# Flamingo block on one core: queries from a feature-major x, LayerNorm's factor applied after the product, and the bias added over two score banks at once

## The reference, cut to what matters

```python
x = x + tanh(g_xattn) * attention(layernorm(x), ctx, ctx, bias, Wq, bq, ..., Wk, ..., Wv, ...)
x = x + tanh(g_ffn) * experts(layernorm(x), Wg, bg, W1, b1, W2, b2)

layernorm(x) = (x - mean(x)) / sqrt(var(x) + 1e-5)          # over the 256 features
q = (layernorm(x) @ Wq' + bq) / 4;  k = ctx @ Wk' + bk;  v = ctx @ Wv' + bv     # LoRA merged into W'
scores = q @ k.T + bias          # bias: 16 heads x 128 x 128 for each sequence
p = softmax(scores);  out = p @ v
```

## Time and profile before

| | |
|---|---|
| time, median of 3 runs | 1283.33 us (1281.91 to 1287.55) |
| span of the profiled execution, first to last instruction | 1282.7 us |
| TensorE busy | 1264.4 us (99%) |
| VectorE busy | 1098.7 us (86%) |
| GpSimd busy | 1034.5 us (81%) |
| ScalarE busy | 860.4 us (67%) |
| mean granted TensorE clock | 0.998 |

### The profile page before, as it was taken

How to read it: one execution, slowest core, us unless ns; L and a number is a source line. 1 busy time by engine, 2 the same in 40 slices (tenths; PEclk the granted TensorE clock), 3 DMA queues, 4 the chain that set the end, 5 groups by cost and what they waited for, 6 DMA issues and landing times. The chain is left out here.

```text
span 1282.7 us, 42229 instructions
## 1 busy us (share of the span) xinstructions
PE 1264.4 (99%) x12820; PEld 1078.7 (84%) x12820; DVE 1098.7 (86%) x2504; ACT 860.4 (67%) x1916; POOL 1034.5 (81%) x1179
## 2 busy tenths in 40 slices
PE   8999999999999999999999999999999999999997
PEld 7888888888888888888888888888887788888886
DVE  6899999999999999999999999999999856665655
ACT  4777777777777777777777777777776533333332
POOL 4879989999999999999999999989988755544545
PEclk9999999999999999999999999999999999999999
DMA  6655655556655656555555555555655589888885
GB/s 237 213 179 196 193 187 181 188 186 196 191 185 181 186 187 197 191 192 183 181 185 187 195 193 185 181 184 187 192 195 182 187 271 282 281 278 281 276 281 184
DMA packets 110649, 263.48 MB, mean 205 GB/s; under 512 B 15332, under 2 KB 34278, under 8 KB 110464
## 3 DMA queue, kind: packets, MB, share of 16 engines
q1 hardware_dynamic: 96912, 226.76, 56.6%
q0 software_dynamic: 12624, 34.62, 6.9%
q10 hardware_dynamic: 1056, 1.39, 0.3%
HBM read 226.72 MB, written 36.91 MB: 206 GB/s over the span
## 5 line engine op out<-in xcount | busy, mean ns | idle before, releaser
L455 POOL TENSOR_TENSOR sc<-sc,negmax 128x1024 f32<-128x1024 f32 x256 | 482.4, 1901 | 25.6 <-DVE negmax L1029 20.7
L1023 DVE TENSOR_TENSOR sc<-bank,sc 128x512 f32<-128x512 f32 x512 | 328.2, 683 | 12.3 <-PE bank L560 7.5
L1029 DVE TENSOR_REDUCE negmax<-sc 128x8 f32<-128x1024 f32 x256 | 312.4, 1220 | 16.3
L862 ACT ACTIVATE PT<-bank 128x512 f32<-128x512 f32 x512 | 281.1, 607 | 1.7 <-PE bank L585 1.5
L585 PE MATMUL bank<-cst,sc 128*128 128x128 f32 x2048 | 272.6, 276 | 0.0
L585 PEld LDWEIGHTS bank<-cst,sc 128*128 128x128 f32 x2048 | 225.3, 140 | 25.8 <-issue 25.1
L525 POOL DMA_INDIRECT out<-og,ids x120 | 118.8, 990 | 114.7 <-issue 106.6
L856 ACT COPY OT<-bank 128x512 f32<-128x512 f32 x128 | 75.1, 587 | 152.1 <-PE bank L595 152.0
L510 POOL DMA_INDIRECT rows_dram<-x2n,slot_i x128 | 136.5, 1066 | 29.3 <-issue 25.2
L560 PE MATMUL bank<-KT,QT 32*128 32x256 f32 x2048 | 146.6, 400 | 0.6 <-ACT V L904 0.6
L595 PE MATMUL bank<-PT,V 128*32 128x128 f32 x4096 | 137.6, 275 | 0.3 <-issue 0.3
(11 more groups left out here) (148 smaller groups left out, 2052.0 us busy)
## 6 DMA issues: line engine op xcount, KB each, us to landing
sc<-in_bias SPq DMA_DIRECT2D x256, 512.0 KB, 4.9
w_sb<-in_w SPq DMA_DIRECT2D x69, 257.0 KB, 3.9
CT<-in_w SPq DMA_DIRECT2D x69, 256.0 KB, 4.1
xg<-rows_dram SPq DMA_DIRECT2D x63, 272.0 KB, 3.8
x_sb<-in_x SPq DMA_DIRECT2D x128, 128.0 KB, 2.0
CT<-in_ctx_in SPq DMA_DIRECT2D x64, 256.0 KB, 5.4
rows_dram<-x2n,slot_i POOLq DMA_INDIRECT x128, 3.8
out<-og,ids POOLq DMA_INDIRECT x120, 4.0
```

Source lines behind the costliest of these rows:

```text
L455: nc.gpsimd.tensor_tensor(s, s, m, ALU.add).then_inc(sub_ok, 1)
L862: nc.scalar.activation(PT[:, t.slot(2), 512 * q:512 * q + 512], turn_bank(t, q)[:], ACT.Exp).then_inc(pt_ready, 1)
L1023: nc.vector.tensor_tensor(s, b_s[q][:], s, ALU.add).then_inc(s_used, 1)
L1029: nc.vector.tensor_reduce(negmax[:, t.slot(2), 8 * h:8 * h + 8], sc[:, t.slot(4), 1024 * h:1024 * h + 1024].rearrange("p (h k) -> p h k", ...
```

## The change

- x is given a second time, feature-major (`x_turned`), and SP loads it straight into `XT`, one transfer of 256 KB for each pair of sequences. ScalarE's first `normalise`, TensorE's two transposes of `xn` and ScalarE's copy to `XT` go.
- The mean is taken out by the weights: once, at the start, the column means of the merged Wq are subtracted from it (two products with ones, one VectorE instruction).
- The factor rs of each token goes through DRAM: `send_scale` writes 128 numbers, `spread_scale` reads them back broadcast over the 128 partitions into `RS`. VectorE's new `scale_queries` multiplies the queries' product by it, from PSUM into `QT`, two instructions of 128x256 for each pair of sequences, behind the residual `x2` in even steps. ScalarE's `queries` then adds the bias in place, as the last thing in its step.
- `add_bias` works on two banks at once (`two[h]`, 128x1024): two instructions in a step in place of four.
- The values' product goes to bank 6. The scores of odd steps wait for `scaled_ok`, that is for `scale_queries` of the step before.

```diff
+            def send_scale(t):
+                sp.wait_ge(rs_ok, t.n(1, 1))
...
+                sp.dma_start(rs_dram[t.n()], ln[:, (t.k - 7) % 8, 0, 0:1]).then_inc(rs_out, 16)
+
+            def spread_scale(t):
+                pair = t.k // 2 % 2
...
+                sp.wait_ge(rs_out, t.n(16, 16))
...
+                sp.dma_start(RS[:, pair, tok:tok + P], rs_rows[t.n()].partition_broadcast(P)).then_inc(rs_in[pair], 16)
...
                 if cur:
                     pe.wait_ge(v_evac, val.n() if val else N)
+                    if ky and ky.slot(2) == 0:
+                        pe.wait_ge(scaled_ok, ky.per(2, 1, 1))
...
-                    pe.wait_ge(xt_evac, qry.n(1, 2))
+                    pe.wait_ge(xT_in[qry.k // 2 % 2], qry.per(4, 16, 16))
                     project("q", qry, XT[:, qry.k // 2 % 2], q_ready)
...
-                    if cur:
-                        pe.wait_ge(s_used, cur.n(4, 3))
-                    elif val.reached(1):
+                    if not cur and val.reached(1):
                         pe.wait_ge(v_evac, val.n())
                     for c in range(KC):
-                        ins = mm(b_v[:, 0:HID], CT[:, pair, c, tok:tok + P], W["v"][:, c, :],
+                        ins = mm(b_v, CT[:, pair, c, tok:tok + P], W["v"][:, c, :],
                                  start=(c == 0), stop=(c == KC - 1))
...
-                    for c in range(KC):
-                        ins = nc.tensor.transpose(b_x[:, c * P:c * P + P],
-                                                  xn[:, nxt.slot(2), c * P:c * P + P], ident)
-                    ins.then_inc(xt_ready, 1)
...
+                act.wait_ge(scaled_ok, t.per(2, 1, 1))
                 for o in range(KC):
-                    act.wait_ge(q_ready, t.per(2, KC, o + 1))
-                    ins = nc.scalar.activation(QT[:, pair, o, :], b_s[o][:, 0:2 * P],
+                    ins = nc.scalar.activation(QT[:, pair, o, :], QT[:, pair, o, :],
                                                ACT.Identity, bias=bq_col[:, o:o + 1])
...
-                dve.wait_ge(s_ready, t.n(4, q + 1))
-                s = sc[:, t.slot(4), 512 * q:512 * q + 512]
-                nc.vector.tensor_tensor(s, b_s[q][:], s, ALU.add).then_inc(s_used, 1)
+                dve.wait_ge(s_ready, t.n(4, 2 * h + 2))
+                s = sc[:, t.slot(4), 1024 * h:1024 * h + 1024]
+                nc.vector.tensor_tensor(s, two[h][:], s, ALU.add).then_inc(s_used, 2)
...
+            def scale_queries(t):
+                pair = t.k // 2 % 2
+                dve.wait_ge(rs_in[pair], t.per(4, 32, 32))
+                for o in range(KC):
+                    dve.wait_ge(q_ready, t.per(2, KC, o + 1))
+                    ins = nc.vector.tensor_tensor(QT[:, pair, o, :], b_s[o][:, 0:2 * P], RS[:, pair, :], ALU.mult)
+                ins.then_inc(scaled_ok, 1)
...
+                        if qry and qry.slot(2) == 0:
+                            scale_queries(qry)
```

More of the change, by code:

```diff
@@ L193, in flamingo_block @@
         inv = sb("inv", [P, 8, HALVES])
-        bank = [ctx.enter_context(nc.psum_tensor(f"bank{i}", [P, 512], F32)) for i in range(8)]
+        two = [ctx.enter_context(nc.psum_tensor(f"two{i}", [P, 1024], F32)) for i in range(2)]
+        bank = [two[i // 2][:, 512 * (i % 2):512 * (i % 2) + 512] for i in range(4)]
+        bank += [ctx.enter_context(nc.psum_tensor(f"bank{i}", [P, 512], F32)) for i in range(4, 8)]
         b_s, b_t = bank[0:4], bank[4:6]
         b_x, b_o = bank[6], bank[7]
-        b_v, b_x2 = b_s[2], b_s[3]
+        b_v, b_x2 = b_x[:, 0:HID], b_s[3]
         o_ps = b_o[:].rearrange("p (h c) -> p h c", c=CELL)
@@ L347, in _ @@
             load(cst[:, 0:C_FIRST], consts[:, 0:C_FIRST], s_id)
+            def send_scale(t):
+                sp.wait_ge(rs_ok, t.n(1, 1))
+                sp.nop(nofuse=True)
+                sp.dma_start(rs_dram[t.n()], ln[:, (t.k - 7) % 8, 0, 0:1]).then_inc(rs_out, 16)
+            def spread_scale(t):
+                pair = t.k // 2 % 2
+                if t.reached(4):
+                    sp.wait_ge(scaled_ok, t.per(2, 1, -1))
+                    sp.nop(nofuse=True)
+                sp.wait_ge(rs_out, t.n(16, 16))
+                sp.nop(nofuse=True)
+                tok = P * t.slot(2)
+                sp.dma_start(RS[:, pair, tok:tok + P], rs_rows[t.n()].partition_broadcast(P)).then_inc(rs_in[pair], 16)
             def step(i, k):
+                behind = seq(i, k, -4)
+                if behind and not (isinstance(i, int) and k < 0):
+                    send_scale(behind)
                 t = seq(i, k, -6) if k > FIRST else None
@@ L548, in _ @@
             pe.wait_ge(s_id, 16)
+            pe.wait_ge(s_cst, 16)
+            pe.wait_ge(s_setd, 3)
+            for c in range(KC):
+                ins = mm(bank[SETUP_BANKS[1]][:, 0:HID], cst[:, C_ONE:C_ONE + P], W["q"][:, c, :],
+                         start=(c == 0), stop=(c == KC - 1))
+            ins.then_inc(s_setc, 1)
             def scores(t):
@@ L586, in turn, with values @@
                 ins.then_inc(tr_ready, 1)
-            def values(t, nxt):
+            def values(t):
                 pe.wait_ge(pt_ready, t.n(4, 4))
-                pe.wait_ge(xt_evac, nxt.n() if nxt else N)
                 if not t.reached(1):
@@ L884, in step @@
                 if old:
[L885 to L887 removed]
+                    normalise(old)
                 if scored:
@@ L895, in step @@
                     copy_rows(early[k - N + 2])
-                if qry and qry.slot(2) == 0:
-                    queries(qry)
                 if ky and ky.slot(2) == 0:
@@ L1095, in step @@
                 if cur:
[L1096 to L1101 removed]
+                    for h in range(2):
+                        add_bias(cur, h)
+                        row_max(cur, h)
                 if here.reached(2) and (gate or done or grp):
@@ L1135, in step @@
                     aggregate(ahead, 0)
+                if qry and qry.slot(2) == 0 and not done:
+                    scale_queries(qry)
                 stats(done, 1)
@@ L1367 @@
     nc = bacc.Bacc("TRN2", target_bir_lowering=False, num_devices=1)
-    order = ["x", "ctx_in", "bias", "wqT", "wkT", "wvT", "bv", "lora_in", "w1", "w2", "b2",
+    order = ["x", "x_turned", "ctx_in", "bias", "wqT", "wkT", "wvT", "bv", "lora_in", "w1", "w2", "b2",
              "consts"]
```

102 lines of the change are left out of this document (49 added, 53 removed).

## The result

The changed kernel takes **2007.8 us** (median of four executions, 2005.3 to 2017.5); the kernel before took 1284.2 on the same chip (1281.9 to 1287.6). The ratio is 1.5645, 95% interval 1.5598 to 1.5692. The forecast was 1330, so the direction was right and 678 us of the 724 were missing from the sum. The profiled execution took 2008.2 us, its span 2006.4.

What follows compares the result with a forecast made beforehand. TensorE and VectorE were taken to share the bound within 1%. Own work +0.7 and waits 2.27 gave +2.97 us per eight steps, times 15.5, plus 2 for the start: 48 on 1282.7, so 1330 us; range given 1295 to 1350.

Steps and rivals of the forecast that it cites:

- Start and transfers: Kernel start and DRAM trip of the factors: +2 us at the start, bounds 0 and 6; in the loop, hidden.
- Rival 3: RS lands late: from 7 us on VectorE waits in every pair, 64 us per further microsecond, 1394 at 8 us; chance 0.06.
- transfers on SP's queue: Sign that the forecast is wrong: transfers on SP's queue appear as a wait of VectorE.
- The round trip: VectorE's scale to TensorE's odd scores to VectorE's next add: 1.35 us, bounds 1.23 and 1.39.
- The wait without routing: VectorE's stall for the scores of odd steps without routing: 0.76 us, in two odd steps of eight.
- With routing: VectorE's stall for odd scores where list_slots fills part of the trip: 0.20 us, in the other two odd steps.
- From odd to even: VectorE's wait between an odd add and the next even one, where TensorE's 7.31 us decides: 0.35 us, once in eight steps.
- The scale: VectorE's scale_queries between residual and statistics: 0.99 us where 0.53 stood, +1.84 in eight steps, bounds 1.6 and 2.2.
- The adds: VectorE's bias adds over two banks: 0.065 us saved a pair, 1.04 us in eight steps, bounds 0.5 and 1.2.
- term of 2 for the start: Centring of Wq and the DRAM trip ahead of the first keys' product: +2 us, bounds 0 and 6.
- Rival 1: TensorE alone is the bound and VectorE has room: 28 us go, 1255 us; chance 0.06.
- Rival 2: The VectorE-TensorE round trip is covered and only VectorE's own work counts: 1296 us; chance 0.08.

Runs made afterwards that it cites:

- e3: e1 with the write of 128 neighbouring 4-byte factors put back on SP's queue, nobody waiting for it or reading it: 1894.1 us.
- e5: e3 with the 128 unread 4-byte pieces put 512 bytes apart in DRAM: 1322.7 us.
- e11: e3 with the 128 unread 4-byte pieces put 64 bytes apart in DRAM: 1324.2 us.
- e6: e3 with 128 unread pieces of 512 bytes in place of 4 bytes, once a step: 1324.3 us.
- e1: The changed kernel without the factors' write to DRAM and SP's wait for it; RS is loaded from ones of the constants: 1321.7 us.
- e8: e1 with the scaling of the queries' product moved ahead of the reciprocal, directly behind the second reduction: 1321.3 us.
- e9: e1 without the scaling on VectorE, the odd scores' wait for it and the load of RS; ScalarE empties the queries' banks: 1274.7 us.
- e10: The kernel before with only the wide adds and the moved banks and wait for ScalarE's copy that they need: 1288.3 us.

## Why the prediction was wrong, point by point

**The step that failed: "Start and transfers".** It said: "In the loop the trip is issued more than a step ahead [...]; transfers land in 2.0 to 5.4 us. Hidden." Rival 3 had the trip late, by itself, at "64 us for each further microsecond" and 0.06. Both took the trip's time as a latency that either fits or doesn't, and priced the write by other transfers. The runs show something else in its place:

- The write has no fixed landing time to be hidden. With its 128 words as neighbours it takes 9.2 to 13.6 us in the chain; with the words 64 or 512 bytes apart it lands in 5.5 and 5.4. The prediction says itself that writes of 4 bytes a partition are not in the trace of before; it bounded the landing by the rows of that trace all the same.
- While it runs, the others run slow too: the x transfer 11.0 us instead of 2.0, GpSimd's scatter 9.3 instead of 3.8. In e3, where the unread write costs 572 us, a step lasts as long as GpSimd's scatter behind the write, not as long as VectorE's work.
- With the trip read back, SP waits for its own write at L365, 126 times. That ties the bias tables and the next write to it. Wait and read back together are 114 us more. The prediction named "transfers on SP's queue" as a wait of VectorE among what would show it wrong, and it came (356.1 us for x, 218.2 for `RS`); it didn't ask what stands behind that wait in SP's order.
- TensorE's clock at 0.835 lengthens what stands on the path, for instance the scores behind a late scale from 1.15 to 2.09 us. How many of the 686 us come by way of the clock was not measured.

That neighbouring words are taken one after the other, each time reading and rewriting the same stretch, would fit all of this, but it is argued and not shown; no run looks inside. The Trainium skill (DMA: Bandwidth & Descriptors, Specifications), which the prediction cited, says that pieces under 512 B are read, changed and written. The runs don't bear out size alone as a price: e5's and e11's 4-byte pieces cost no more than e6's 512-byte ones (1322.7, 1324.2, 1324.3 us). Distances between 4 and 64 bytes were not tried, nor was the trip with spaced words and its readback.

**The rest of the forecast** can be read from e1: 1321.7 against 1330, eight steps 64.04 us (571.74 to 635.78) against 64.7. The seams stand in VectorE's timeline of e1 nearly as worked out:

```profile
578.97 1.23 DVE L1035 TENSOR_TENSOR sc<-two,sc 128x1024 f32<-128x1024 f32 x1 [0.20 <-PE two L592]
...
603.65 1.23 DVE L1035 TENSOR_TENSOR sc<-two,sc 128x1024 f32<-128x1024 f32 x1
...
611.06 1.22 DVE L1035 TENSOR_TENSOR sc<-two,sc 128x1024 f32<-128x1024 f32 x1 [0.47 <-PE two L592]
...
617.26 0.74 DVE L1100 TENSOR_TENSOR QT<-two,RS 128x256 f32<-128x256 f32 x2
617.92 0.41 DVE L1056 BATCH_NORM_STATS2 st<-x 128x6 f32<-128x256 f32 x1
...
619.33 1.22 DVE L1035 TENSOR_TENSOR sc<-two,sc 128x1024 f32<-128x1024 f32 x1 [0.68 <-PE two L592]
```

And in TensorE's:

```profile
618.06 1.15 PE L592 MATMUL two<-KT,QT 32*128 32x256 f32 x16 [1.15 <-DVE QT L1100]
```

- *The round trip.* Forecast 0.06 + 1.29 = 1.35 us; it is 0.06 (617.26 + 0.74 to 618.06) + 1.27 = 1.33. The wait without routing 0.76, measured 0.68, twice in eight steps. With routing 0.20, measured none (603.65). From odd to even 0.35 once; measured 0.20 and 0.47. Sum 2.03 for 2.27.
- *The scale.* From residual to statistics 0.99 forecast, 1.01 measured (616.91 to 617.92), 1.92 in eight steps for 1.84. Right.
- *The adds.* -1.04 in eight steps. The record is 1.22 as said, the pair saves 0.06, but the wide add's later start behind the aggregation takes more than half of it: 0.05 a step, -0.4 in eight. This term was mis-sized.
- *Not in the sum.* The loop's turn (0.4) falls into a wait for scores; the routing's comparison, 487 ns in the trace of before, is 194 in e1, 0.6 less in eight steps.

With these, -0.4 + 1.9 + 2.0 - 0.4 - 0.6 - 0.1 = +2.4, where +2.31 was measured. 2.31 x 15.5 is 36 us; the first add starts 1.4 us later than before (20.30 against 18.87 us), which makes 37; e1 has 37.5. The forecast's term of 2 for the start had the trip through DRAM in it, which e1 leaves out. That the forecast comes within 8 us of e1 is in part luck: the adds were taken 0.6 us too good in eight steps, and the two things that were not in the sum take 1.0 back. e8 shows a limit of such sums: a wait that is taken away gives time back only where nothing else fills the place.

**The rivals.** Rival 1 (TensorE alone, 1255 us) falls: e9 comes to 1274.7 even without the scaling. What it rests on is half right: in e10, with its transposes, TensorE comes to 62.0 us for eight steps, 0.3 above the 61.7 of before, so wide adds with the moves that they need are worth nothing there. Rival 2 (trip covered, 1296) falls by the 12.2 us of waits for scores in 400 us of e1. Rival 3 was the nearest, and by its rule 11 us of landing would give 1586 us; it lacks the slowing of all the others. The chance of 0.06 that it got was too small, for the rows had nothing to bound such a write by.

## What to carry to other kernels

Before a transfer is called hidden, ask not only whether it lands in time but what it does to the others: read the DMA share beside the GB/s in a stretch, and the landing time of transfers that were not touched. A column of single words from 128 partitions should not be written to neighbouring addresses of DRAM; unread, a distance of 64 bytes was enough here, and one row of 512 bytes was as cheap. Where two engines share the bound within 1%, read a moved instruction at its seam: start behind what, and who waits for its end; a record's own length gave only half of the answer.

## What the runs showed of the hardware that was not expected

- 128 words of 4 bytes into one 512-byte stretch of DRAM, once a step, take the DMA engines from 0.70 busy at 205 GB/s to 0.82 busy at 126 GB/s, against the same packets 512 bytes apart. The small packets keep records of 9 ns; packets of the loads behind them stand for up to 8 us.
- One comparison on 128x32 elements took 194, 354, 487 and 661 ns on average in e1, e9, the kernel before and e8, with its own code unchanged. The other engines stand elsewhere at that moment; which of them it meets, if any, was not isolated.
- An add over two PSUM banks of 512 columns takes 1.22 us, as long as a reduction of 1024 columns in SBUF; one over 512 columns 0.683.
